# Front of a decoder kernel: value and projection weights multiplied first, heads folded in the other order, value side and first queries moved across the stage boundary

## The reference, cut to what matters

```python
# 1 self attention, one head of 128
h = rmsnorm(x) * g;  q, k, v = split(h @ w_qkv + b_qkv)
o = softmax(rope(q) @ rope(k).T * LN3 / sqrt(128)) @ v
x = layernorm(x + (o @ w_proj + b_proj + x))
# 2 cross attention, 16 heads of 64, queries from x, keys and values from the context
q = (layernorm(x) * w2 + b2) @ Wq * (1 + side) + side
k, v = split((layernorm(ctx) * w1 + b1) @ Wkv)
x = layernorm(x + softmax(q @ k.T / 8) @ v @ Wout)
# 3 a product-key feed forward layer over 1024 experts, top 8 for each of 8 heads
```

## Time and profile before

| | |
|---|---|
| median of 3 runs | 1302.22 us (1298.18 to 1302.53) |
| profiled execution | 1300.68 us, span 1299.0 us |
| busy in the span | PE 90%, DVE 88%, ACT 68%, POOL 48% |
| mean granted TensorE clock | 0.903 of full speed |

### The profile page before, as it was taken

The page is one execution under the profiler, slowest core; times in us unless marked ns, Lnnn a source line. Parts: engine busy times, 40 slices in busy tenths (PEclk is TensorE's granted clock), DMA queues, the critical chain, the costliest instruction groups (busy, mean ns, idle before and its releaser), DMA issues. The chain is left out here.

```text
span 1299.0 us, 32706 instructions
## 1 busy us (share of the span) xinstructions
PE 1167.1 (90%) x12762; PEld 905.6 (70%) x12762; DVE 1139.3 (88%) x2858; ACT 885.2 (68%) x1248; POOL 622.2 (48%) x520
## 2 busy tenths in 40 slices
PE   6969999999999999999999999999997748977778
PEld 4746777777767777776777777777776636867678
DVE  7768899998989999899999999998987688999984
ACT  4768888888888888888988888898883422222211
POOL 3226667757566775757677575776331300000000
PEclk9779999999999999999999999999998657656666
DMA  7119999999999999999999999898996200000000
GB/s 176 25 48 204 195 193 195 199 186 192 199 205 201 190 200 187 195 205 195 206 183 200 194 199 198 177 198 165 189 194 147 58 1 1 5 6 5 5 5 6
DMA packets 665394, 186.25 MB, mean 143 GB/s; under 512 B 653939, under 2 KB 662295, under 8 KB 664855
## 3 DMA queue, kind: packets, MB, share of 16 engines
q1 hardware_dynamic: 665238, 184.16, 74.2%
HBM read 19.97 MB, written 0.82 MB: 16 GB/s over the span
## 5 line engine op out<-in xcount | busy, mean ns | idle before, releaser
L1174 PE MATMUL ps<-pT,xa_hi 128*128 128x128 f16 x2288 | 380.8, 217 | 20.7 <-ACT uT L1009 20.7
L986 ACT ACTIVATE e<-ps,bias 128x1444 f32<-128x1444 f32 (+1 forms) x208 | 305.8, 1470 | 128.4 <-DVE bias L1058 127.6
L1178 PE MATMUL ps<-pT,xa_hi 128*128 128x128 f16 x2288 | 380.7, 217 | 1.7 <-DMA pT<-p 1.7
L1175 PE MATMUL ps<-pT,xa_lo 128*128 128x128 f16 x2288 | 380.9, 217 | 0.0
L1056 DVE TENSOR_REDUCE nmax<-ps 128x1 f32<-128x1444 f32 (+1 forms) x208 | 343.9, 1653 | 13.7 <-PE ps L1158 12.6
L1068 DVE TENSOR_TENSOR p<-e,p 128x1408 f16<-128x1408 f32 (+3 forms) x288 | 304.4, 1098 | 41.9 <-ACT p L994 41.0
L994 ACT ACTIVATE p<-e 128x1408 f16<-128x1408 f32 (+1 forms) x208 | 288.2, 1385 | 13.9 <-ACT e L986 0.7
L942 POOL TENSOR_TENSOR p<-e,p 128x1408 f16<-128x1408 f32 (+1 forms) x128 | 196.5, 1556 | 181.4 <-ACT p L994 181.4
L1174 PEld LDWEIGHTS ps<-pT,xa_hi 128*128 128x128 f16 x2288 | 222.1, 98 | 48.8 <-issue 35.9
L1156 PE MATMUL ps<-xT_hi,q_hi 128*128 128x512 f16 (+1 forms) x624 | 229.8, 368 | 4.0 <-POOL q_lo L931 3.3
L1175 PEld LDWEIGHTS ps<-pT,xa_lo 128*128 128x128 f16 x2288 | 222.1, 98 | 12.9
(11 more groups left out here) (237 smaller groups left out, 1929.5 us busy)
## 6 DMA issues: line engine op xcount, KB each, us to landing
raw<-in_ctx SPq DMA_DIRECT2D x16, 704.0 KB
pT<-p SPq DMA_TRANSPOSE x416, 3.7
f_wq<-in_L_ffn_w_q SPq DMA_DIRECT2D x1, 1024.0 KB, 5.3
f_wqt<-in_ffn_wq_t SPq DMA_DIRECT2D x2, 512.0 KB, 6.7
raw<-in_ctx SPq DMA_DIRECT2D x48, 18.0 KB
x_tok<-in_x SPq DMA_DIRECT2D x4, 200.0 KB
out_x<-ost SPq DMA_DIRECT2D x6, 128.0 KB, 1.9
wk_t<-in_wk_t SPq DMA_DIRECT2D x1, 512.0 KB, 8.2
```

The lines of the kernel that those rows point to most:

```text
L986: act.activation(e32[t % E_BUF][rows, :], score_banks(t)[rows, 0:T], ACT.Exp, bias=bias[rows, t % N_BUF:t % N_BUF + 1]).then_inc(e_done, 1)
L1174: pe.matmul(out, hi, ph, start=n == 0, stop=False)
L1175: pe.matmul(out, lo, ph, start=False, stop=False)
L1178: pe.matmul(out, hi, pl, start=False, stop=False)
```

## The change

The change touches only `front` and the first slots of `cross`, and one operation for each batch in `cross`.

1. Value times projection: `w_vp` = wv times w_proj / 2 is made once (one product on PE, one copy on ACT), and the bias goes into `bp_row`. Then `values` gives the projected values, and `oT_out` and `projected` go. The division by the row sums moves behind the product: `weights` and `doubled` go, POOL's `biased` makes x plus the bias row, and DVE's `residual(c)` does one multiply-add for each batch.
2. Head folding in the other order: keys times `fold_k` first (`keys_folded`, two heads to a product), copied once (`kf_out`, two copies in place of four), then times wq (`queries_folded`).
3. The value side leaves `front`: `values_folded` and `values_out` stand on PE in tiles 1, 2 and 3 of `cross`, with their copies on ACT. `once_normed` goes; POOL's `first_normed(b)` makes that value in slot 2 of each batch.
4. The queries of batch 0 are made in `front`: `first_queries` on PE, `q0_out` and `q0_hi_out` on ACT, `q0_lo` on POOL. The `q` jobs of batch 0 leave `cross`.
5. `queries_lo`, `sc1` and `kb` move from DVE to POOL. The statistics of context 1 move to the start of `cross`, its normalisation from there into tiles 1 to 3. On SP `w_proj` and `bp_row` are loaded ahead of the last two token groups. The lists of all engines are written in a new order.

The lists of the front after the change, cut to what the steps below speak of:

```diff
@@ sync
             sp.dma_start(cols[:, :], a["att_cols"]).then_inc(ld_w, 16)
+            sp.dma_start(w_proj[:, :], a["L0_attn_w_proj"]).then_inc(ld_late, 16)
+            sp.dma_start(bp_row[:, :], ...).then_inc(ld_late, 16)
             tokens_in(2)
             tokens_in(3)
@@ gpsimd
+            pool.wait_ge(bp_done, 1)
+            biased(0)
             context_rstd(pool, cx, nhalf, first)
+            biased(1)
+            biased(2)
+            biased(3)
+            norm_rstd(0)
+            queries_lo(0)
+            norm_rstd(1)
             context_lo(pool, cx, first)
-            norm_rstd(0)
-            norm_rstd(1)
+            queries_lo(1)
+            pool.wait_ge(ld_side, 16)
+            pool.tensor_scalar(sc1[:, :, :], side[:, :, :], 1.0, 1.0 / QA_SCALE, ALU.add, ALU.mult).then_inc(kb_done, 1)
+            pool.wait_ge(kbar_done, 1)
+            pool.tensor_tensor(out=kb[:, :, :], in0=side[:, :, :], in1=kbar..., op=ALU.mult).then_inc(kb_done, 1)
             norm_rstd(2)
+            q0_lo(0)
+            queries_lo(2)
             norm_rstd(3)
-            context_rstd(pool, cx, nhalf, second)
+            q0_lo(1)
+            q0_lo(2)
+            queries_lo(3)
+            q0_lo(3)
@@ scalar (the list after)
+            hT_out(1)
+            act.wait_ge(vp_ps, 1)
+            act.activation(w_vp[:, :], ps[:, 3, 0:D], ACT.Copy, scale=0.5).then_inc(vp_done, 1)
+            tokens_scaled(2)
+            hT_out(2)
+            v_out(0)
+            tokens_scaled(3)
+            hT_out(3)
             exponents(0)
             v_out(1)
             probT_out(0)
-            oT_out(0)
             context_norm_act(act, cx, first, 0)
             exponents(1)
...
+            qa_hi_out(0)
             probT_out(3)
             qa_hi_out(1)
             queries_hi(1)
+            q0_out(0)
+            q0_hi_out(0)
+            qa_hi_out(2)
             twice_normed(2)
             qa_hi_out(3)
+            q0_out(1)
+            q0_hi_out(1)
             queries_hi(2)
+            q0_out(2)
+            q0_hi_out(2)
             twice_normed(3)
+            q0_out(3)
+            q0_hi_out(3)
             queries_hi(3)
@@ vector (the list after)
+            context_stats(dve, cx, first, 0)
+            context_stats(dve, cx, first, 1)
             maxima(0)
             rotated(1, 0)
             rotated(1, 1)
+            context_stats(dve, cx, first, 2)
+            context_stats(dve, cx, first, 3)
             maxima(1)
             rotated(2, 0)
+            residual(0)
             rotated(2, 1)
+            context_shift(dve, cx, first)
             stats(0)
             maxima(2)
             rotated(3, 0)
             shifts(0)
+            residual(1)
             rotated(3, 1)
             stats(1)
             queries_out(0)
             maxima(3)
             shifts(1)
+            residual(2)
             dve.wait_ge(ld_k, LD_K)
             dve.tensor_reduce(ksum[:, :], wk_d[:, :, :], AX_X, ALU.add).then_inc(bp_done, 1)
             stats(2)
             queries_out(1)
             qa_lo_out(0)
             context_mix(dve, cx, first)
             shifts(2)
+            residual(3)
             qa_lo_out(1)
             stats(3)
@@ tensor (the end of the list after)
+            keys_folded(1)
+            pe.wait_ge(bp_done, 2)
+            pe.wait_ge(ln_done, 1)
             pe.matmul(bank(0, D, (H,)), fold_k[:, :], ksum[:, :], start=True, stop=True).then_inc(kb_ps, 1)
+            queries_folded(0)
             ln_turned(1)
+            queries_folded(1)
             prob_turned(3)
             weighted(3)
+            first_queries(0)
+            first_queries(1)
             ln_turned(2)
+            first_queries(2)
             ln_turned(3)
+            first_queries(3)
@@ new functions
+            def residual(c):
+                dve.wait_ge(exp_done, (c + 1) * G)
+                dve.reciprocal(rc[:, of(c)], rs[:, of(c)]).then_inc(stats_chain, 1)
+                dve.wait_ge(y_ps, c + 1)
+                dve.wait_ge(x2b_done, c + 1)
+                dve.wait_ge(stats_chain, 5 * c + 1)
+                for j in range(G):
+                    b = c * G + j
+                    ins = dve.scalar_tensor_tensor(out=z[:, b, :], in0=bank(c, S, (G, D))[:, j, :], scalar=rc[:, b:b + 1],
+                                                   in1=z[:, b, :], op0=ALU.mult, op1=ALU.add)
+                ins.then_inc(stats_chain, 1)
+            def first_queries(g):
+                pe.wait_ge(qa_lo_done, 2 if g < 2 else 4)
...
+            def queries_lo(c):
+                pool.wait_ge(ln_split, c + 1)
+                pool.tensor_tensor(out=ln_lo[:, tok(c)], in0=lnT[:, tok(c)], in1=ln_hi[:, tok(c)], op=ALU.subtract).then_inc(ln_lo_done, 1)
@@ cross, vector and scalar
-            for part in range(3):
-                context_norm(dve, cx, Batch(None, 1), part)
+            for part in range(4):
+                context_stats(dve, cx, Batch(None, 1), part)
...
+                if 1 <= t <= 3:
+                    context_norm(dve, cx, Batch(None, 1), t - 1)
...
-            take_queries(0, 0)
-            queries_hi(0, 0)
...
+                if t == G_SLOT:
+                    values_folded_out(0)
+                    values_folded_out(1)
+                if t in W2_SLOTS:
+                    values_out_out(2 * W2_SLOTS.index(t))
+                    values_out_out(2 * W2_SLOTS.index(t) + 1)
```

More of the change, by code:

```diff
@@ new lines, in queries_folded @@
+            def queries_folded(k):
+                pe.wait_ge(rot_chain, rot_count(NG - 1, 1))
+                pe.wait_ge(kf_done, k + 1)
+                for j in range(4):
+                    for half in range(2):
+                        r, rows = 4 * k + j, slice(half * DH, (half + 1) * DH)
+                        last = pe.matmul(qa_bank(2 * k + half)[:, j, :], wq_t[rows, r, :], kf[rows, r, :], start=True, stop=True)
+                        if j == 3:
+                            last.then_inc(qa_ps, 1)
@@ L961, in _ @@
                     low_half(t)
+                if i == X1_SLOT and b < B:
+                    first_normed(b)
                 for kind, of, g in jobs_of(t):
@@ L1180, in values, with values_folded, values_out @@
                 last.then_inc(pv_done, 1)
-            job("q", 0, 0)
+            def values_folded(k):
+                if k == 0:
+                    pe.wait_ge(ld_v, 32)
+                for j in range(4):
+                    r = 4 * k + j
+                    last = pe.matmul(ps[:, 6 + k, j * D:(j + 1) * D], wv_d[:, 2 * r:2 * r + 2, :].rearrange("d h e -> d (h e)"),
+                                     fold_v[:, :], start=True, stop=True)
+                last.then_inc(fv_ps, 1)
+            def values_out(k):
+                pe.wait_ge(fv_done, 2 * k + 2)
+                for j in range(4):
+                    for half in range(2):
+                        r, rows = 4 * k + j, slice(half * DH, (half + 1) * DH)
+                        last = pe.matmul(ps[:, 6 + half, j * D:(j + 1) * D], gv[rows, r, :], wout[rows, r, :], start=True, stop=True)
+                        if j == 3:
+                            last.then_inc(fv_ps, 1)
             for t in range(ALL_TILES + DRAIN):
@@ L1852, in decoder @@
             "kb": sb("kb", [D, B, H], F32, part),
-            "x1": sb("x1", [S, B, D], F32, part),
+            "z": sb("z", [S, B, D], F32, part), "x_mv": sb("x_mv", [S, B, 2], F32, part), "x_rs": sb("x_rs", [S, NG, 2, G], F32, part),
+            "q32": sb("q32", [D, HQ], F32, part),
+            "q_hi": [sb(f"q_hi{i}", [D, HQ], F16, part) for i in range(2)],
+            "q_lo": [sb(f"q_lo{i}", [D, HQ], F16, part) for i in range(2)],
+            "fold_v": sb("fold_v", [D, D], F32, part), "wv_d": sb("wv_d", [D, H, DH], F32, part), "wout": sb("wout", [P, H // 2, D], F32, part),
+            "ld_v": whole.enter_context(nc.semaphore("ld_v")),
         }
```

436 lines of the change are left out of this document (203 added, 233 removed).

## The result

| | before | after |
|---|---|---|
| median of 4 runs each, same chip | 1302.38 us (1298.18 to 1303.04) | 1317.01 us (1313.42 to 1317.74) |
| profiled execution | 1300.68 us, span 1299.0 us | 1313.42 us, span 1311.7 us |
| cross begins | 78.0 us | 93.5 us |

The ratio is 1.0123, with a 95% interval of 1.0105 to 1.0142: the change costs 14.6 us. The profiled execution of after happens to be the fastest of its four, so sizes are better read from positions inside the span. I use three: where cross begins, and how long after that exponent(5) and exponent(13) start. Before, these are 77.98, +31.85 and +68.12 us. After, they are 93.47, +30.47 and +67.33. So the front is 15.49 us longer, the first tiles give 0.79 back by tile 13, and 14.70 remain.

A forecast was written before the change was run, and what follows sets the result against it. The front was taken as bound by waits in in-order lists, cross by its tiles' pace. 1300.7 + 10.4 (longer front) - 2.3 (first tiles of cross) = 1308.8 us profiled, given as 1310 for the median; range 1298 to 1318.

The forecast's parts named there:

- (a): Start of the front: ACT must copy w_vp first, and maxima(0) starts at 23.3 us, before 21.68.
- (b): Front: DVE runs full, context_shift is late, and ACT's exponents(1) behind it comes at 36.3 us, before 29.76.
- (c): Front: PE's prob_turned(1) waits for exponents(1), next products at half clock; maxima(2) at 42.1 us (40.4 at full clock).
- (d): Front: POOL's norm_rstd(1) stands behind queries_lo(0) and starts at 51.1 us, before 47.29; ksum on DVE ends at 55.2.
- (f): Front: POOL does queries_lo(1), sc1 and kb before norm_rstd(2), which comes at 65.9 us, before 52.58.
- (h): End of front: POOL's norm_rstd(3) at 78.65 us, before 63.76; cross begins near 88.4, 10.4 us later than before.
- (i): First tiles of cross: exponent(0) at +5.5 us after cross begins, before +9.6; exponent(5) at +29.5, before +31.8.
- gain of the ramp: First tiles of cross: exponent(5) comes sooner after cross begins, a gain of 2.3 us (1 to 4).
- (e): Front: PE waits for ksum with queries_folded behind; at half clock queries_folded(0) takes 3.3 us, products through prob_turned(3) reach 61.8.
- The waits are milder: Rival: PE keeps its full clock through the front's pauses, front ends near 83.3 us, total 1305; chance 30%.
- The shorter tail wins: Rival: with the value side gone from its tail, the front ends at 73 us, total 1295; chance 15%.
- POOL becomes a bound: Rival: first_normed is not hidden in cross, 0.3 us or more per batch add 5, 1315 or above; chance 5%.

The follow-up runs named there:

- e4_all: The changed kernel with the edits of e1_ctx_early, e2_pool_order, e5_kb_late and e3_load_late together; median 1296.43 us, ratio 0.9968 to the kernel before.
- e6_tail: e4_all with context_mix behind stats(3), shifts(3) ahead of qa_lo_out(2), first_queries(3) ahead of ln_turned(3); median 1294.22 us, ratio 0.9955.
- experiment 9: e8_slots with POOL's context_lo moved to just ahead of norm_rstd(3) and DVE's context_mix behind the third qa_lo_out; median 1292.96 us, ratio 0.9945.
- e5_kb_late: The changed kernel with PE's key-sum product behind both queries_folded and ACT's kbar copy behind twice_normed(1); one execution 1308.14 us.
- e3_load_late: The changed kernel with SP's load of context 3 in cross behind the transposes of tile 3, not tile 0; one execution 1313.55 us.
- Experiments 1 to 3: In this order e1_ctx_early, e2_pool_order and e5_kb_late, each one edit to the changed kernel; 1310.38, 1306.54 and 1308.14 us in one execution each.
- experiment 4: The run e3_load_late: the changed kernel with SP's load of context 3 issued later in cross; one execution 1313.55 us.
- e1_ctx_early: The changed kernel with DVE's context_stats parts 2 and 3 ahead of maxima(0), context_shift after rotated(1,1); one execution 1310.38 us.
- e2_pool_order: The changed kernel with POOL's norm_rstd(1) ahead of queries_lo(0), norm_rstd(2) ahead of context_lo, norm_rstd(3) ahead of q0_lo(0); one execution 1306.54 us.
- e7_warm: The changed kernel with unread PE products in two pauses, 26 ahead of prob_turned(1), 19 ahead of the key-sum wait; one execution 1314.97 us.
- e8_slots: e6_tail with the value folding one tile earlier in cross (G_SLOT 0, W2_SLOTS 1 and 2); median 1292.48 us, ratio 0.9948.
- e10_tokens_first: The kernel of experiment 9 with SP issuing tokens_in(2) and tokens_in(3) ahead of w_proj and bp_row again; median 1291.13 us, ratio 0.9927.

## Where the prediction held and where it failed

The direction, the range and the mechanism held: waits in in-order lists, not work. The size was off: 7.8 us were forecast and 14.6 measured, near the top of the range (1318). Step by step, with the time from the step before in brackets:

| step | predicted | measured | difference added here |
|---|---|---|---|
| (a) maxima(0) | 23.3 | 23.97 | +0.7 |
| (b) exponents(1) | 36.3 (13.0) | 38.54 (14.57) | +1.6 |
| (c) maxima(2) | 42.1 (5.8) | 44.05 (5.51) | -0.3 |
| (d) norm_rstd(1) | 51.1 (9.0) | 53.26 (9.21) | +0.2 |
| (d) key sum ends | 55.2 (4.1) | 57.56 (4.30) | +0.2 |
| (f) norm_rstd(2) | 65.9 (10.7) | 68.90 (11.34) | +0.6 |
| (h) norm_rstd(3) | 78.65 (12.75) | 81.70 (12.80) | 0 |
| (h) cross begins | 88.4 (9.75) | 93.47 (11.77) | +2.0 |
| (i) exponent(5), gain of the ramp | 2.3 | 1.38 | +0.9 |
| (i) the gain at tile 13 | 2.3 | 0.79 | +0.6 more |

**The terms that failed are the stretched DVE steps in (b) and (h) and the gain of the ramp in (i).** The front's misses sum to 5.1 us (93.47 - 88.4). Of these 2.7 are two DVE instructions: the addition of (b), 1.65 us in place of 0.57, and shifts(3) of (h), 1.79 in place of 0.15. The prediction saw the first, named it with the Trainium skill's rule, put "up to 1.2 us" on it (it was 1.08) and left it out of the sum. Among the unknown prices it looked for the second from the wrong side: it asked whether DVE would hold up POOL's subtractions, "as DVE is mostly waiting". POOL's took 0.94 us each, the low end, but a DVE that wakes for a tiny step on the path is held for all that POOL has begun. The Trainium skill, SBUF — State Buffer, section "SBUF: two separate sides", says that whichever of a GpSimd operation that reads SBUF and a DVE operation with two SBUF inputs starts first gets the pair for the whole instruction, and that the other fully blocks. The trace agrees with it in the addition and in shifts(3) of after, in `context_mix` of e4_all and in shifts(2) of e6_tail, and experiment 9 by moving the subtraction. It shows more than that section says: shifts(3) was not let in between two subtractions that follow each other on POOL (83.30 to 84.24 and 84.20 to 85.14), so it lost 1.64 us and not 0.9.

The 0.7 us of (a) are scatter. I had called the two early loads nothing: "Their scaling on ACT starts 2 us later than before anyway, so this costs nothing". That held. The squares of tokens 2 waited 3.30 us for their transfer, but in e5_kb_late, where they start later still (11.04), maxima(0) is at 22.99. What differs is PE's products for queries_keys(0,1), in after and in e3_load_late:

```profile
13.32 1.59 PE L477 MATMUL ps<-hT,w_all 128*128 128x400 f32 x2
14.70 1.27 PE L478 MATMUL ps<-hT,w_all 128*128 128x400 f32 x2
```

```profile
13.21 0.86 PE L477 MATMUL ps<-hT,w_all 128*128 128x400 f32 x2
13.91 0.83 PE L478 MATMUL ps<-hT,w_all 128*128 128x400 f32 x2
```

ACT's copy of `w_vp`, its scaling and with them maxima(0) follow at 1.2 us less. Step (c) takes most of that back (6.42 us in e3_load_late in place of 5.51), so that 0.3 us reach the start of cross.

The other 1.7 us are spread over the steps, none above 0.6. Step (e) is worse than the table shows. Its prices do not add up: with queries_folded(0) at 3.3 us, ln_turned(1), queries_folded(1) and prob_turned(3) can't take 2.7 together. Measured were 2.08 us for each queries_folded and 4.94 for the three steps behind the first, 1.17 of it a wait for twice_normed(1), which ACT does behind `context_hi` (1.47 us), a copy that the walk left out of the front. POOL's sc1 then took 0.40 us in place of 0.9, below both ends given for it. That only 0.6 us is left of all this is luck.

**Experiments 1 to 3 bear out the walk's own steps**: the stall before exponents(1) (7.2 us), POOL's powers behind its subtractions (6.9), the key sum ahead of the folding products (4.9), each within 0.3 us of what was expected for the start of cross when undone alone. They overlap: 16.4 us together with the edit of experiment 4.

**The ramp.** The direction held and exponent(0) came at +5.73 (predicted 5.5). Predicted for exponent(5) was +29.5, measured +30.47. The gain of 2.3 us measured 1.38 at tile 5 and 0.79 at tile 13. The walk had no fall of the clock behind the first tiles. In each of the five profiled kernels with cross in the order of after (after, e1_ctx_early, e2_pool_order, e5_kb_late, e7_warm) it falls once or twice from 12 to 34 us after cross begins, in windows of 2 us to 0.50 to 0.57 at the lowest, and none of them reaches +29.5. In e8_slots and e9_lo_later it stays up, and they have +28.15. That this explains the whole of the missing gain is not shown, as in before it falls too (0.50 and 0.70, 18 to 22 us after cross begins). The walk also followed PE, DVE and ACT and not the sync queue, where the moved normalisation holds the load of context 3 and behind it the transposes of tile 1 until 116.85. Undoing that gave 0.57 us at tile 5 and 1.04 at tile 13, within the scatter.

**The rivals.** "The waits are milder" fell: the clock was at 0.50 after the pauses of (c) and (e), and with the first of them filled and the second in part cross still begins at 91.3. "The shorter tail wins" was given its condition, norm_rstd(2) and (3) as early as before and a front end below 73.5, and the runs show that this is what decides: with them at 50.31 and 59.62 (e4_all) the kernel is faster. Its cross begins 0.9 us earlier than before, not 4.7; only e9_lo_later and e10_tokens_first, with 4.0 and 4.4, come near that. "POOL becomes a bound" fell: its additional 11.7 us in cross are hidden, and the distance to before does not grow from tile 13 to 182.

**From front to total.** 15.49 - 0.79 = 14.70 us at tile 13, measured 14.6 between the medians. That these agree so closely is luck, as the profiled pair differs by 12.7. The prediction's sum on this scale was 8.1.

Open: what decides whether and where the clock falls in the first tiles of cross. It differs between kernels whose lists are the same there, and no run took it apart.

## What to carry to other kernels

A front bound by waits is changed by the order of its lists before it is changed by their work: the same operations cost 14.6 us in one order and gained 6 to 8 in another, and the three places that did it were each a long or late instruction ahead of a short one that others waited for. When walking new lists, walk every queue, the one that issues the DMAs too, and put the powers and shifts that release the next group ahead of subtractions that only feed the end. Where GpSimd works on SBUF, give VectorE's small steps on the path a place where GpSimd is idle; moving only one of them hands the block to the next, and what it returns is what the next wait leaves, 0.7 of 2.3 us here. Before pricing a small edit from one profile, look at how far kernels with the same lists in that stage differ: here up to 1.5 us at the first maxima and 1.8 us at exponent(5).

## What the runs showed of the hardware that was not expected

- A VectorE operation on 100x4 values took 2.48 us in place of 0.15 (e6_tail) beside two GpSimd subtractions that follow each other, one of 128x1536 values that ended at 55.62 and one of 128x400 that ended at 56.53; it ended at 56.54. The variance step, one SBUF input of 100x4, took 1.24 us in place of 0.17 (e9_lo_later) and ended within 0.03 us of the subtraction of 128x1536. Another operation of that kind, `nb` in e4_all, was let in between two: it took 1.15 us and ended at 24.66, where the first `biased` ended at 24.63 and the second at 25.86.
- Not held were, in the 3.10 us of the same subtraction in e9_lo_later, the statistics over z (100x128, 57.00), which took their usual 0.86 us for four, and a subtraction with an operand in PSUM (128x512, 56.40), which took 0.68; and in after the four multiply-adds with an operand in PSUM at 32.98, which took their usual 1.13 beside `biased`. GpSimd can be the one that is held: where VectorE's addition got in behind a first `biased` in e1_ctx_early and ended at 25.75, the second took 1.61 us in place of 1.27.
- PE's clock did not stay up behind the 19 added products: it was at 1.00 from 56 to 58 us, at 0.69 in the next 2 us and at 0.50 from 60 us. The pause before the key sum was filled but for 1.05 us, and PE stood 2.09 us more for twice_normed(1) right behind it.
- In all twelve profiled executions PE's first two pairs of products over 400 columns take 1.67 and 1.54 us, where later pairs take 0.86 and 0.83, and the profile shows the granted clock at 1.00 there. From when on they take the shorter time differs, and with it maxima(0): 22.63 us in e2_pool_order, 24.15 in e8_slots.
- A delay in the front of 14.7 us reached the end of cross 195 tiles later as 14.2: nothing in the steady part takes up a late start.
